# Loading the down weights early, and the first LayerNorm on VectorE, in a holographic attention and FFN layer on eight cores

## The reference

```
x = x + layernorm(attn(layernorm(x)))
x = x + layernorm(ffn(layernorm(x)))

attn(x): bound     = circular convolution of x with bind_key
         hologram  = decay_matrix @ bound        (d ** (t - s) for s <= t, d = sigmoid(decay))
         retrieved = circular correlation of hologram with unbind_key
         return x + gate * retrieved
ffn(x):  h = silu(x @ wg.T) * (x @ wu.T)         (3072 hidden channels)
         return h @ wd.T
```

## Time and profile before

| | |
|---|---|
| median of three runs | 850.31 us |
| profiled execution, time / span of the slowest core (7) | 849.73 / 848.2 us |
| TensorE matmuls busy | 676.5 us, 80% |
| VectorE busy | 237.1 us, 28% |
| ScalarE busy | 228.0 us, 27% |
| start and key product, to the first scan matmul | 0 to 77.8 us |
| scan | 77.8 to 141.9 us |
| first FFN half, 24 steps | 272.9 to 480.1 us |
| second FFN half, 24 steps | 584.4 to 751.8 us |

### The profile page before, as it was taken

How to read it: one execution, slowest core, us unless ns; L and a number is a source line. 1 busy time by engine, 2 the same in 40 slices (tenths; PEclk the granted TensorE clock), 3 DMA queues, 4 the chain that set the end, 5 groups by cost and what they waited for, 6 DMA issues and landing times.

```text
span 848.2 us, 8420 instructions; the slowest of 8 cores (835.4 to 848.2 us)
## 1 busy us (share of the span) xinstructions
PE 676.5 (80%) x3024; PEld 298.4 (35%) x3024; DVE 237.1 (28%) x579; ACT 228.0 (27%) x325; POOL 29.9 (4%) x60
## 2 busy tenths in 40 slices
PE   0196888996105995995978999789999999999994
PEld 0043223442003442342433444344444444444441
DVE  0282000555572127110211122233211111112223
ACT  2036552444414212110111122424112212202222
POOL 1000000000000000000000000000000000000000
PEclk9998555999655998897997999879999999999998
DMA  9960000000020249366483401001444444400111
GB/s 199 209 206 1 0 1 1 1 0 1 0 50 1 50 75 144 66 102 110 75 133 66 76 26 50 25 26 51 100 75 77 75 81 77 83 7 26 51 50 75
DMA packets 12441, 53.40 MB, mean 63 GB/s; under 512 B 1408, under 2 KB 1408, under 8 KB 11760
## 3 DMA queue, kind: packets, MB, share of 16 engines
q0 software_dynamic: 7792, 36.08, 25.0%
q1 hardware_dynamic: 4608, 16.78, 5.6%
HBM read 80.12 MB, written 8.39 MB: 104 GB/s over the span
## 4 chain that ended last, share of the span: by engine, by line
PE 69%; DMA 11%; ACT 7%; DVE 6%; issue 6%; POOL 0%; DVEq 0%; ACTq 0%; POOLq 0%
PE pg L627 19%; PE pu L635 18%; PE pu L708 10%; PE pf L708 10%; DMA wgu<-wgu 6%; DMA cubb<-cuT 4%; PE pb L356 4%; PE cp L234 4%; ACT t1a L431 2%; DVE sqd L410 2%; ACT xw L313 2%; PE pt L570 2%; ACT t1a L403 1%; PE pb L351 1%; DVE x2t L574 1%
## 5 line engine op out<-in xcount | busy, mean ns | idle before, releaser
L627 PE MATMUL pg<-x2t,wgu 128*128 128x512 bf16 x768 | 182.4, 393 | 34.7 <-DMA wgu<-wgu 29.7
L635 PE MATMUL pu<-x2t,wgu 128*128 128x512 bf16 x768 | 173.6, 379 | 0.0
L652 ACT ACTIVATE sil<-pg,z 128x512 bf16<-128x512 f32 x96 | 65.4, 687 | 271.3 <-PE pg L627 271.3
L627 PEld LDWEIGHTS pg<-x2t,wgu 128*128 128x128 bf16 x768 | 76.2, 100 | 134.9 <-issue 53.5
L635 PEld LDWEIGHTS pu<-x2t,wgu 128*128 128x128 bf16 x768 | 75.1, 98 | 90.6
L658 DVE SCALAR_TENSOR_TENSOR xw<-sil,pu 128x512 bf16<-128x512 bf16 x64 | 43.6, 687 | 184.7 <-PE pu L635 182.6
L473 PE MATMUL pr<-hc,zt 128*128 128x512 bf16 x256 | 62.6, 389 | 7.7 <-ACT t1a L403 6.8
L570 PE MATMUL pt<-idb_s,x2s 128*128 128x128 bf16 x128 | 15.9, 302 | 58.7 <-ACT x2s L560 45.5
L234 PE MATMUL cp<-cubb,cbtb 128*128 128x512 bf16 x128 | 30.1, 401 | 39.9 <-DMA cubb<-cuT 39.9
L708 PE MATMUL pf<-wdtb,xw 128*128 128x512 bf16 x256 | 57.9, 379 | 2.1 <-DVE hc L658 2.1
L708 PE MATMUL pu<-wdtb,xw 128*128 128x512 bf16 x256 | 59.4, 386 | 0.0
(11 more groups left out here) (91 smaller groups left out, 449.5 us busy)
## 6 DMA issues: line engine op xcount, KB each, us to landing
wgu<-wgu POOLq DMA_DIRECT2D x48, 512.0 KB, 5.6
x<-xin SPq DMA_DIRECT2D x16, 512.0 KB, 34.9
out<-x SPq DMA_DIRECT2D x16, 512.0 KB, 2.6
wdtb<-wdt POOLq DMA_DIRECT2D x3, 2048.0 KB, 20.2
cbtb<-cbt POOLq DMA_DIRECT2D x1, 2048.0 KB, 22.6
cubb<-cuT POOLq DMA_DIRECT2D x1, 2048.0 KB, 35.9
cstf_s<-cstf POOLq DMA_DIRECT2D x1, 257.0 KB, 7.7
cstb_s<-cstb POOLq DMA_DIRECT2D x1, 128.0 KB, 8.2
```

Source lines behind the costliest of these rows:

```text
L627: pe_g[eta][c] = op("tensor", lambda e, sl=sl, c=c, d=d: e.matmul(PG[sl][:, 512 * c:512 * c + 512], WGU[sl][:, 128 * d:128 * d + 128], X2T ...
L635: pe_u[eta][c] = op("tensor", lambda e, sl=sl, c=c, d=d: e.matmul(PU[sl][:, 512 * c:512 * c + 512], WGU[sl][:, 1024 + 128 * d:1024 + 128 * ...
L652: sc_sil[eta][c] = op("scalar", lambda e, sl=sl, c=c: e.activation(SIL[sl][:, 512 * c:512 * c + 512], PG[sl][:, 512 * c:512 * c + 512], AF ...
```

## The change

The load of wdt becomes one transfer, issued by GpSimd after cuT, behind a wait for all 16 loads of x; the three issues in the FFN loop go. The sixteen norms of `emit_x1_norm` move from ScalarE to VectorE, as a multiplication and an addition with per-partition scalars, and TensorE waits for them on VectorE's semaphore.

```diff
     wt_ccin = dma("gpsimd", CUBB[:], cuT[:, :], "WCC")
-    wt_wd = 3 * 16
+    for gname in ("LDX", "LDX2", "LDX3", "LDX4"):
+        w("gpsimd", gname, 64)
+    wt_wd = dma("gpsimd", WDTB[:], wdt[:, :], "WWD")
...
     def emit_x1_norm(t):
-        w("scalar", "DV", dv_ln1)
-        sc_x1[t] = op("scalar", lambda e, t=t:
-                      e.activation(XW[t][:], X[t][:], AF.Identity,
-                                   bias=NB1c[:, t:t + 1], scale=R1c[:, t:t + 1]), "SC")
+        w("vector", "DV", dv_ln1)
+        sc_x1[t] = op("vector", lambda e, t=t:
+                      e.tensor_scalar(XW[t][:], X[t][:], R1c[:, t:t + 1], NB1c[:, t:t + 1],
+                                      ALU.mult, ALU.add), "DV")
...
     for I in range(NCH):
-        w("tensor", "SC", sc_x1[4 * I + 3])
+        w("tensor", "DV", sc_x1[4 * I + 3])
...
                 dv_ln2_done = emit_ln2(1, dv_ln2_done)
-            if hf == 0 and eta in (7, 13, 19):
-                g = (7, 13, 19).index(eta)
-                dma("gpsimd", WDTB[:, 8192 * g:8192 * g + 8192],
-                    wdt[:, 8192 * g:8192 * g + 8192], "WWD")
```

## The result

The changed kernel takes 818.54 us, the median of 8 runs (817.26 to 819.45), against 850.07 us before (8 runs, 848.29 to 852.43): ratio 0.9627, 95% interval 0.9614 to 0.9640. The gain is 31.5 us. The forecast was 810.8 us with a range of 803 to 817, so the direction was right and the size was missed by 8 us. The profiled execution took 818.53 us, its slowest core is core 4.

The account below looks back on a forecast made before the run. TensorE, busy for 80% of the span, was taken to be stalled by wgu queued behind wdt pieces. 848.2 - 37.7 - 1.8 = 808.7 us of span, 810.2 with 1.5 around it, forecast 810.8, range 803 to 817.

Parts of the forecast that it names:

- The holes are wdt's, the early load is free.: First FFN half: wdt pieces delay wgu, making holes of 9.35, 9.43 and 8.59 us; early wdt load costed at zero.
- What is late next is wgu itself: First FFN half without the wdt holes: wgu is the next thing late, with some 0.7 us slack per step.
- I take 1.5 us for the first half, between 0 and 5: First FFN half: idle time left by late wgu after the early wdt load, 1.5 us, between 0 and 5.
- the first part: Early load of wdt, first FFN half: gain of 37.7 us (34 to 39).
- The rival of wgu with the cores in step: FFN halves: wgu landings lengthen and become the bound; 830 us, up to 848; chance 0.06.
- The norms: Scan: norms on VectorE 0.7 us each, start 1.4 us later, holes 1.73 us; net -1.8 us, between -3.0 and +0.3.
- The cores come together: Whole kernel: spans of the cores within some 4 us of each other after the change.
- The range: Whole kernel: the forecast's own range 807 to 816 us; with nearer rival cases, 803 to 817 us.
- The rival of the clock: Scan: shorter holes let TensorE stay at full clock; up to 20 us go, 790 to 804 us; chance 0.10.
- may not hold: Scan, argument against full clock: the clock never rose during 13.6 us of unbroken matmuls in chunk 1.

Follow-up runs that it names:

- small pieces: Kernel before with norms on VectorE, statistics spread, wdt loaded in the first FFN half as 24 pieces, one behind each wgu: 809.53 us, ratio 0.9513.
- only wdt early: Kernel before with only the load of wdt made early, the x1 norms staying on ScalarE: 822.90 us, ratio 0.9662.
- norms only: Kernel before with only the x1 norms moved to VectorE, wdt staying in the FFN loop: 844.73 us, ratio 0.9916.
- spread statistics: Changed kernel with the second half's LayerNorm statistics dealt out, one tile in each of steps 6 to 13: 810.61 us, ratio 0.9518.
- filled ones: Changed kernel with statistics spread and eight unread matmuls after each chunk's state matmuls, in the holes between chunks: 790.72 us, ratio 0.9324.
- the kernel with the state matmuls in the middle: Changed kernel with statistics spread, a chunk's eight state matmuls after its fifth group, and a second state row: 784.60 us, ratio 0.9221.

## Why the prediction was right or wrong

*The holes are wdt's, the early load is free.* Right, but of the first hole only 3.7 us were wdt's alone. The load goes out at 58.14 and lands at 100 us; the time with wdt in small pieces is the same, and the first halves are no shorter.

*"What is late next is wgu itself".* Wrong, and this is the step that failed. Next late at step 8 was the block of statistics on VectorE, with silu behind it on ScalarE. I read the holes' releasers in the earlier trace rows, which name only what came last, and took the difference of busy and idle time between the halves as all wdt's, though the halves differ in a second thing, the statistics, which only the first one computes. The term "I take 1.5 us for the first half, between 0 and 5" leaves out 5.45 us of hole and 6.10 - 3.61 = 2.5 us of restart. From the first gate matmul to the down projection the slowest core takes 179.1 us, instead of 208.2 on core 7 before (272.91 to 481.11, where that kernel starts the projection). So the first part gained 29.1 us and not 37.7. Spread over the steps the statistics cost nothing and the term is right: 170.4 us on the slowest core, 37.8 less than 208.2, and 810.21 us in the profile, 810.61 us in the median, where the forecast said 810.8. In the earlier trace rows nothing warned of it. The timeline of VectorE in the trace of before did: the block's multiplications end at 337.4, which left 3.7 us of the first hole to gain and not 9.35.

*The rival of wgu with the cores in step.* Not seen: 5.2 to 6.5 us on core 4.

*The norms.* Right in its parts: 0.73 us a norm, forecast 0.7; the first scan matmul 1.8 us later (79.54 against 77.78), forecast 1.4, of which 0.3 us is that VectorE's scalings of hc begin later on this core (73.24 against 72.95); holes 1.82 to 1.84, forecast 1.73, released by the state update. The retrieval starts at 139.33 instead of 142.2, 2.9 us earlier, forecast 1.8; the rest lies in chunk 2, which began at the full clock (108.07 to 109.8 on core 4) where the kernel before had it for 0.1 us only (109.30 to 109.4 on core 7). The Trainium skill, "VectorE: DVE Perf Modes", section on the perf-mode tier table, gives fp32 tensor_scalar two elements a cycle, and the estimate from it was 0.69 us; the trace shows 0.73 us with f32 in and bf16 out.

*The cores come together.* Wrong, they went apart, from 12.8 to 20 us. The part of it that wdt made is gone (only wdt early: 816.6 to 821.3), and the scan's clock made a new one.

*The range.* The bounds of the two parts, 34 to 39 and -3.0 to +0.3, add up to 808 to 817 us, not to the 807 to 816 that I wrote. Neither holds 818.54.

*The rival of the clock.* It had a chance of 0.10 as an event of all cores. It happened on some, in part of the scan. With holes of 1.8 us in four kernels (changed, norms only, spread statistics, small pieces), 13 of 32 core executions kept the full clock through at least one of chunks 1 to 3; with a first hole of 3.76 us in three kernels, none of 24 did; without holes or with filled ones, all of 24 kept it from its rise in chunk 0 to the retrieval. Its price, up to 20 us, was about right: without the holes 26.0 us go (810.61 to 784.60), 5.5 of them the holes themselves. I argued that the scan's mix of matmuls "may not hold" the clock. It holds it for 37 us, once it is granted. What it does not do is bring it up: in 56 core executions of the seven kernels with holes, after chunk 0 the clock never rose during the eight groups of a chunk, only during the eight state matmuls or at most 0.3 us behind them. The earlier trace rows show the 13.6 us at 0.50 and not the rise that followed at 106.0.

Which cores keep the clock at 1.8 us goes with how early it had risen in chunk 0, and so with how long it took from the first scan matmul to the first matmul behind the first hole. That is 88.83 - 79.25 = 9.58 us on core 3 and 89.14 - 79.54 = 9.60 us on core 4 of the changed kernel. The 32 executions fall into four groups that do not overlap:

| from the first scan matmul to the end of the first hole | executions | full clock |
|---|---|---|
| 9.44 to 9.58 us | 6 | kept through the first hole and chunk 1 |
| 9.60 to 9.64 us | 5 | kept through none of chunks 1 to 3 |
| 9.72 to 9.86 us | 7 | lost after the first hole, back before the second, kept through it and chunk 2 |
| 10.79 to 11.05 us | 14 | kept through none of chunks 1 to 3 |

The clock had risen 2.6 to 2.9 us behind the first scan matmul in the first group, 3.0 in the second, 3.2 to 3.5 in the third and 5.4 to 5.9 in the fourth. Why the moment of the rise decides, and what sets it on a core, no run here shows. Nor do the counts separate the length of the hole from that moment.

## What to carry to other kernels

When a stall goes, list all that was running under it, on every engine, and ask which of it ends last; of two stalls that lie over each other, the shorter is worth nothing alone and the longer only what it stands above the other. Here the statistics alone gave 0 us and wdt alone 28.4 us (851.29 to 822.90), both together 34.1 us (844.73 to 810.61, with the norms on VectorE). A block of small work that belongs to a later stage can be dealt out over steps with slack, and so can a large transfer in a shared queue. Where the time is that of the slowest core, a hole that only sometimes costs the clock has its full price: remove it, or fill it.

## What was not expected of the hardware

The granted clock of TensorE rose in chunk 0 and, where it was not lost in a hole, lived on through chunks whose mix of matmuls did not bring it up in 13.6 us at the lower level. After it had fallen in the scan it came back only with the state matmuls at the end of a chunk: on core 3 of the changed kernel at 112.9 us, 0.8 us into them. Two cores whose rise in chunk 0 differed by some hundredths of a microsecond could end 14 us apart at the retrieval (cores 3 and 4). At 2.4 GHz a chunk with its state matmuls takes 9.5 us, from the first matmul of chunk 1 to that of chunk 2 in the kernel with the state matmuls in the middle (timeline of its slowest core):

```profile
88.94 0.37 PE L354 MATMUL pb<-dpb,sqd 1*128 1x512 bf16 x1
...
98.47 0.39 PE L354 MATMUL pb<-dpb,srowb 1*128 1x512 bf16 x1
```

At 1.2 GHz it takes 17.1 us (108.07 - 89.14, less the hole of 1.82, on core 4 of the changed kernel). And matmuls whose result nobody reads, put into idle time, made the kernel 16 to 20 us faster.
